# Shifted-window attention block on one core: three placements changed inside the eight-round loop

## Chip, cores and metric

One Trainium2 chip, one core. The metric is the device time of one execution in microseconds (us); lower is better.

## What is computed

The reference is a Swin block on x of 32 x 56 x 56 x 64 floats: LayerNorm, roll by (-3, -3), windows of 7 x 7, eight-headed attention with a position bias and the shift mask, projection, roll back, residual; then LayerNorm, fc1 to 256, GELU, fc2, residual.

```python
y = roll(_ln(x, norm1_w, norm1_b), (-3, -3))           # windows of 49 tokens, 64 channels
q, k, v = split(win @ qkv_w.T)                         # 8 heads of 8
attn = softmax(q @ k.T * scale + bias + mask)
x = shortcut + roll_back(attn @ v @ proj_w.T + proj_b)
z = gelu(_ln(x, norm2_w, norm2_b) @ fc1_w.T + fc1_b) @ fc2_w.T + fc2_b
return x + z
```

## The kernel before, in words

The work is cut into 128 units (NSB). A unit is 16 windows: two rows of eight, the two rows lying in partitions 0 to 48 and 64 to 112. Every engine runs a `body(i, m)` over i with an inner loop of eight rounds, `k` = 0 to 7. A round is one pair of windows per partition half. The order inside a round is written out by hand, and every engine keeps its own order strictly; semaphores tie the engines together. The rest of the block (norms, projections, the MLP) is spread over the eight rounds, each piece for another unit: in pass i the scores are those of unit i; `a` = i+1 has its q, k and v made, `f` = i+2 has its normalised rows turned, `n` = i+3 has its first norm begun; `c` = i-1 has its attention output finished and projected, `d` = i-2 has its second norm, `e` = i-3 its MLP, `g` = i-4 its result.

TensorE (PE), in each round: `scores` (L722, with mask matmuls L726 in some rounds) into the one bank S; `scores_T` (L738) into ST; the extra piece of the round; `shift` (L744), which adds the negated row maxima to ST; `times_v` (L758); in round 4 then `fc2` (L851). The extra pieces: round 0 `project_qk` (L784), round 1 `project_v` (L798), round 2 `fc1_low` and round 3 `fc1_high` (both L829), round 4 `turn_y` (L766, "M<-weights,y"), round 5 `turn_o` (L766, "M<-weights,on"), round 6 `project_out` (L814); at the top of the next round 0 `turn_z` (L766) and `turn_back` (L859). I write S(k) for the first score matmul of round k, and sh(k), V(k) for `shift` and `times_v` of round k.

VectorE (DVE), in each round: `neg_max` (L582), the negated maxima nm of S. PE may write S(k+1) only after nm(k). Extra pieces: round 0 `ln2_sum`, `normalise` of heads (L588, L592), `evac_zT`, then nm, `result` (L634), `ln2_center` (L612); round 1 `low_parts` (L573) and `ln2_var` (L617, L621); round 2 `ln1_sum` (L546); round 3 `ln1_center` (L553); round 4 `normalise` of the second half ahead of nm, then `evac_yT`; round 5 `ln1_var` (L558, L562); round 6 `add_attention` (L600).

GpSimd (POOL), in each round: `shift_rows` (L326), which spreads nm into nmd; sh(k+2) waits for it. Extra: round 0 `keep_residual` (L346) ahead of it, round 1 `ln1_rows` (L339), round 4 `ln2_rstd` and `ln2_rows` (L353, L359), round 7 `ln1_rstd` (L333).

ScalarE (ACT), in each round: `exp` (L426). Extra: round 0 `high_parts` (L407) and `square2`, round 1 `place_v` (L417), round 2 both halves of GELU (L445, with a table load on each side), round 3 `square1`, round 4 `evac_oT`, round 5 `evac_m`.

SyncE issues the DMAs: x in, results out, and per unit sixteen copies of hl into the per-head tiles qp and kp (L274), which the next scores read.

Of the kernel before, what the change touches and what calls it, by code (L numbers as in the profile page):

```python
# [43 lines left out]
def swin_block(nc, x, c_vec, c_weights, c_projb, c_keys, c_diag, c_shift, out):  # L44
    NSB = x.shape[0]
    ctx = ExitStack()
    with ctx:
# [6 lines left out]
        def sem(name):  # L54
            return ctx.enter_context(nc.semaphore(name))
# [127 lines left out]
        s_g = sem("s_g")  # L183
# [12 lines left out]
        def on_chip(u):  # L196
            return not isinstance(u, int) or 0 <= u < NSB

        def later(u, k=1):
            return not isinstance(u, int) or u >= k  # L200
# [11 lines left out]
        def at_unit(i, k, back):  # L212
            return i + (k - back) // U, (k - back) % U
# [271 lines left out]
        def _(dve):  # L485
# [41 lines left out]
            def gather_heads():  # L527
                dve.wait_ge(c_tb, 1)
                then(V.tensor_copy(first[:], S[0:W0 + HEADS, 0:N]))
                for src, lo, hi in ((S[0:W0 + HEADS, N:10 * N], 0, 9), (ST[0:W0 + HEADS, 0, 0:10 * N], 9, 19),  # L530
                                    (ST[0:W0 + HEADS, 1, 0:5 * N], 19, 24)):
                    part = V.tensor_tensor(heads[:, lo:hi, :], src.rearrange("h (k q) -> h k q", q=N),
                                           first[:].unsqueeze(1).broadcast_to([W0 + HEADS, hi - lo, N]), ALU.subtract)
                    part.then_inc(c_heads, 1)

            def place_bias(n, b):
                dve.wait_ge(c_rows_in, 32)
                then(V.tensor_copy(bias_hi[:], bias_t[:]))
                V.scalar_tensor_tensor(bias_rows[:], bias_hi[:], lopart[0:BIAS], bias_t[:], ALU.mult, ALU.add).then_inc(c_bias, 1)
                dve.wait_ge(c_bias, 1)  # L540
                V.tensor_copy(qp[n][b][0:BIAS].rearrange("p h (w q) -> p h w q", q=N),
                              bias_rows[:].unsqueeze(2).broadcast_to([BIAS, HEADS, 8, N])).then_inc(c_q[n][b], 1)

            def ln1_sum(u, r):
                dve.wait_ge(s_x[r % RING], loaded(u, r))
                V.tensor_reduce(sum1[:], xin[r % RING][:], AX_X, ALU.add).then_inc(s_sum1, 1)  # L546
# [24 lines left out]
            def low_parts(u):  # L571
                dve.wait_ge(s_hi, u + 1)
                V.tensor_tensor(hl[:, 1].rearrange("m b a t -> m a b t"),  # L573
                                M[:, 0:2, 0:HT].rearrange("m a (b t) -> m a b t", b=2),
                                hl[:, 0].rearrange("m b a t -> m a b t"), ALU.subtract).then_inc(s_lo, 1)
# [9 lines left out]
            def normalise(u, b):  # L585
                dve.wait_ge(s_pv, U * u + 4 * b + 4)
                o = O[0:R, 0:PAIRS * 4 * VC].rearrange("r (a f) -> r a f", f=VC)
                V.reciprocal(rec[:], o[:, :, 2 * D:VC]).then_inc(s_rec, 1)  # L588
                dve.wait_ge(s_rec, 2 * u + b + 1)
                if b == 0 and later(u):  # L590
                    dve.wait_ge(s_oTp, u)
                V.tensor_tensor(on[:, PAIRS * b:PAIRS * b + PAIRS, :].rearrange("r p (h e d) -> r (p h) e d", e=2, d=D),  # L592
                                o[:, :, 0:2 * D].rearrange("r a (e d) -> r a e d", d=D),
                                rec[:].unsqueeze(3).broadcast_to([R, 4 * PAIRS, 2, D]), ALU.mult).then_inc(s_on, 1)
# [8 lines left out]
            def ln2_sum(u, r):  # L603
                dve.wait_ge(s_att, u + 1)
                V.tensor_reduce(sum2[:], xres[r % RING][:], AX_X, ALU.add).then_inc(s_sum2, 1)
# [9 lines left out]
            def ln2_var(u):  # L615
                dve.wait_ge(s_sq2, u + 1)
                V.tensor_reduce(ss2[:], sq2[:], AX_X, ALU.add).then_inc(s_ss2, 1)  # L617
                dve.wait_ge(s_ss2, u + 1)
                if later(u):
                    dve.wait_ge(s_rs2, u)  # L620
                V.tensor_scalar(veps2[:], ss2[:], 1.0 / C, EPS, ALU.mult, ALU.add).then_inc(s_ve2, 1)  # L621
# [15 lines left out]
            def body(i, m):  # L637
                a, f, n, c, d, e, g = i + 1, i + 2, i + 3, i - 1, i - 2, i - 3, i - 4
                if isinstance(i, int) and i == -2:
                    gather_heads()  # L640
                if isinstance(i, int) and i == 0:
                    place_bias(0, 0)
                for k in range(U):
                    if k == 0:
                        if on_chip(d):
                            ln2_sum(d, m + 2)
                        if on_chip(c):
                            normalise(c, 0)
                        if on_chip(e):
                            evac_zT(e)  # L650
                    if k == 4 and on_chip(c):
                        normalise(c, 1)
                    if on_chip(i):
                        neg_max(i, k)
                    if k == 0:
                        if on_chip(g):
                            result(g, m)
                        if on_chip(d):
                            ln2_center(d, m + 2)
                    if k == 1:  # L660
                        if on_chip(a):
                            low_parts(a)
                        if on_chip(d):
                            ln2_var(d)
                    if k == 2 and on_chip(n):
                        ln1_sum(n, m + 3)
                    if k == 3 and on_chip(n):
                        ln1_center(n, m + 3)
                    if k == 4 and on_chip(f):
                        evac_yT(f)  # L670
                    if k == 5 and on_chip(n):
                        ln1_var(n)
                    if k == 6 and on_chip(c):
                        add_attention(c, m + 3)
# [4 lines left out]
        def _(pe):  # L679
# [121 lines left out]

            def turn_o(u, e, a):
                pe.wait_ge(s_on, 2 * u + 2)
                if not on_chip(e):
                    pe.wait_ge(s_vx, 2 * a + 2)
                turn_tokens(3, on, s_oTp)

# [55 lines left out]
            def body(i, m):  # L863
                a, f, c, d, e, g = i + 1, i + 2, i - 1, i - 2, i - 3, i - 4
                if i == -2:
                    pe.wait_ge(c_weights_in, 16)
                    pe.wait_ge(c_scaled, 1)
                if i == 0:
                    pe.wait_ge(c_const_in, 48)
                for k in range(U):  # L870
                    u2, j2 = at_unit(i, k, 2)
                    r2 = m if k >= 2 else m + 3
                    u4, j4 = at_unit(i, k, 4)
                    r4 = m if k >= 4 else m + 3
                    if k == 0 and on_chip(e):
                        turn_z(e, g, i)
                    if k == 0 and on_chip(g):
                        turn_back(g)
                    if i == -2 and k in (0, 5) or i == 0 and k in (2, 3, 5, 6, 7):
                        keep_running(1)  # L880
                    if i == -1 and k == 5:
                        keep_running(5)
                    if on_chip(i):
                        scores(i, m, k)
                    if k == 1 and on_chip(a):
                        room_for_v(a, e, g)
                    if on_chip(u2):
                        scores_T(u2, r2, j2)
                    if k == 0 and on_chip(a):
                        project_qk(a, d)  # L890
                    if k == 1 and on_chip(a):
                        project_v(a)
                    if k == 2 and on_chip(e):
                        fc1_low(e, a, d)
                    if k == 3 and on_chip(e):
                        fc1_high(e, a, g)
                    if k == 4 and on_chip(f):
                        turn_y(f, e)
                    if k == 5 and on_chip(c):
                        turn_o(c, e, a)  # L900
                    if k == 6 and on_chip(c):
                        project_out(c, f)
                    if on_chip(u2):
                        shift(u2, r2, j2)
                    if on_chip(u4):
                        times_v(u4, r4, j4)
                    if k == 4 and on_chip(e):
                        fc2(e)
# [92 lines left out]
```

## Time and profile before

| what | value |
|---|---|
| median of 3 runs | 2191.48 us (2190.91 to 2192.81) |
| the profiled execution | 2191.34 us, its span 2189.5 us |
| PE matmul busy | 2140.3 us (98%) |
| DVE busy | 1780.1 us (81%) |
| POOL busy | 1772.9 us (81%) |
| ACT busy | 1545.3 us (71%) |
| DMA engines | 28% by the one large queue |
| mean granted TensorE clock | 0.993 of 2.4 GHz |

The trace is read as follows. A row of the timeline is a start, a duration, the engine, the line and the tiles, with a count where neighbours of one kind are merged. A matmul's recorded duration contains the time in which it drains beside its follower, so lengths of pieces on PE are taken from start to start. A row may also contain time in which the instruction had begun but was held. Three engines are over 80% busy, so a wait moved on one of them soon meets a wait of another.

### The profile page before, as it was taken

To read this page: it belongs to the slowest core of one execution; us is meant where nothing else is said; L and a number is where in the kernel's file an instruction comes from. 1 tells how busy PE (TensorE), PEld (TensorE's weight loads), DVE (VectorE), ACT (ScalarE), POOL (GpSimd) and SP (SyncE) were. 2 spreads that over 40 slices of the span, in tenths; PEclk is the share of its full clock that TensorE was granted. 3 is DMA by queue.
4 is the path that set the end of the run, shared out by engine and by line. 5 is a ranking of instruction groups with operands and counts; after the bars stand their busy time and mean duration, and the time that the engine had idled before them with its cause. 6 is when DMAs were issued, how large, how long until landed. Compare 5 with 4: busy or idle time off the path is not lost.

```text
span 2189.5 us, 148006 instructions
## 1 busy us (share of the span) xinstructions
PE 2140.3 (98%) x62790; PEld 1667.7 (76%) x62790; DVE 1780.1 (81%) x3231; ACT 1545.3 (71%) x2435; POOL 1772.9 (81%) x1687
## 2 busy tenths in 40 slices
PE   6999999999999999999999999999999999999997
PEld 3777777777777777777777777777777777777775
DVE  5788888888888888888888888888888888888874
ACT  4577777677677777767777776776777777777774
POOL 5788888888888888888888888888888888888874
PEclk8999999999999999999999999999999999999999
DMA  4232233222323332232323223233223333322321
GB/s 111 65 78 78 75 75 76 77 77 76 79 74 76 76 76 77 75 79 76 77 76 76 77 75 77 78 75 79 75 77 77 76 77 76 77 76 76 77 70 32
DMA packets 178587, 165.86 MB, mean 76 GB/s; under 512 B 21144, under 2 KB 152458, under 8 KB 178074
## 3 DMA queue, kind: packets, MB, share of 16 engines
q1 hardware_dynamic: 178074, 157.60, 28.0%
q8 instruction: 495, 8.11, 1.6%
q14 instruction: 18, 0.15, 0.0%
HBM read 28.99 MB, written 25.77 MB: 25 GB/s over the span
## 4 chain that ended last, share of the span: by engine, by line
PE 88%; DVE 4%; issue 3%; ACT 2%; SPq 2%; DMA 1%; DVEq 0%; POOL 0%; ACTq 0%; POOLq 0%
PE O L758 14%; PE S L722 11%; PE ST L744 10%; PE M L766 9%; PE ST L738 9%; PE M L829 9%; PE M L851 8%; PE M L814 5%; PE M L798 5%; PE M L784 4%; PE M L859 2%; PE S L726 2%; SPq L274 1%; DVE nm L582 1%; ACT gl L445 1%
## 5 line engine op out<-in xcount | busy, mean ns | idle before, releaser
L326 POOL TENSOR_TENSOR nmd<-diag,nm 121x392 f16<-121x392 f16 x1024 | 900.3, 892 | 288.1 <-DVE nm L582 234.1
L582 DVE TENSOR_REDUCE nm<-S 121x8 f16<-121x392 f32 x1024 | 574.3, 561 | 225.7 <-PE S L722 138.3
L426 ACT ACTIVATE pT<-ST 113x392 f32<-113x392 f32 x1024 | 506.9, 496 | 229.7 <-PE ST L744 224.9
L758 PEld LDWEIGHTS O<-vx,pT 113*49 113x49 f32 x16384 | 548.6, 126 | 45.1 <-issue 6.1
L758 PE MATMUL O<-vx,pT 113*49 113x18 f32 x16384 | 522.2, 196 | 3.8 <-issue 1.9
L722 PE MATMUL S<-kp,qp 128*49 128x49 f16 x16384 | 390.7, 186 | 11.0 <-DVE nm L582 7.9
L738 PE MATMUL ST<-qp,kp 128*49 128x49 f16 x16384 | 387.0, 185 | 2.4 <-issue 2.3
L722 PEld LDWEIGHTS S<-kp,qp 128*49 128x49 f16 x16384 | 313.0, 103 | 93.1 <-issue 55.5
L744 PE MATMUL ST<-nmd,shiftw 121*49 121x392 f16 x2048 | 354.4, 342 | 0.2 <-POOL nmd L326 0.2
L738 PEld LDWEIGHTS ST<-qp,kp 128*49 128x49 f16 x16384 | 324.8, 103 | 10.2 <-issue 2.3
L407 ACT ACTIVATE hl<-M 128x784 f16<-128x784 f32 x128 | 105.5, 824 | 309.1 <-PE M L784 229.3
L744 PEld LDWEIGHTS ST<-nmd,shiftw 121*49 121x49 f16 x2048 | 108.7, 102 | 246.8 <-issue 122.5
L346 POOL TENSOR_TENSOR xres<-xin,projb 113x512 f32<-113x512 f32 x128 | 205.2, 1603 | 78.6 <-DVE res L634 78.5
L829 PE MATMUL M<-zT,weights 64*128 64x392 f32 x1024 | 237.9, 540 | 2.0 <-DVE zT L627 1.5
L445 ACT ACTIVATE gl<-M,vec 128x784 f32<-128x784 f32 x256 | 220.0, 911 | 4.0 <-PE M L829 2.5
L353 POOL TENSOR_TENSOR rstd<-veps,mhalf 113x8 f32<-113x8 f32 x128 | 210.8, 1647 | 13.9 <-DVE veps L621 13.9
L333 POOL TENSOR_TENSOR rstd<-veps,mhalf 113x8 f32<-113x8 f32 x128 | 209.7, 1638 | 10.5 <-DVE veps L562 10.5
L851 PE MATMUL M<-gl,weights 128*64 128x392 f32 x1024 | 195.1, 503 | 4.9 <-ACT gl L445 4.9
L417 ACT ACTIVATE vx<-M 49x512 f32<-49x512 f32 x256 | 154.8, 605 | 17.1 <-PE M L798 4.6
L426 ACT ACT_TABLE_LOAD x126 | 161.7, 1283 | 2.2
L445 ACT ACT_TABLE_LOAD x126 | 161.7, 1283 | 2.2
L600 DVE TENSOR_TENSOR xres<-M,xres 113x512 f32<-113x512 f32 x128 | 88.6, 692 | 72.7 <-PE M L814 72.7
(90 smaller groups left out, 3369.2 us busy)
## 6 DMA issues: line engine op xcount, KB each, us to landing
qp<-hl SPq DMA_DIRECT2D x1024, 49.0 KB
kp<-hl SPq DMA_DIRECT2D x1024, 49.0 KB
xin<-in_x SPq DMA_DIRECT2D x256, 98.0 KB
out<-res SPq DMA_DIRECT2D x256, 98.0 KB
kp<-in_c_keys SPq DMA_DIRECT2D x4, 588.0 KB, 7.2
weights<-in_c_weights SPq DMA_DIRECT2D x1, 448.0 KB, 4.4
bias_t<-spread SPq DMA_DIRECT2D x2, 73.5 KB, 2.2
shiftw<-in_c_shift SPq DMA_DIRECT2D x1, 139.0 KB
```

Source lines behind the costliest of these rows:

```text
L326: nc.gpsimd.tensor_tensor(nmd[j % LAG][:], diag[:], nm[j % LAG][:].unsqueeze(2).broadcast_to([RM, 2 * 4, N]), ALU.mult).then_inc(s_nmd, 1)
L333: nc.gpsimd.tensor_tensor(rstd1[:], veps1[:], mhalf[:], ALU.pow).then_inc(s_rs1, 1)
L353: nc.gpsimd.tensor_tensor(rstd2[:], veps2[:], mhalf[:], ALU.pow).then_inc(s_rs2, 1)
L426: nc.scalar.activation(pT[j % LAG][:].rearrange("k w h q -> k (w h q)"), ST[0:R, j % 2, 0:HK], ACT.Exp).then_inc(s_e, 1)
L445: nc.scalar.activation(gl[:, c], M[:, 2 * c:2 * c + 2, 0:HT], ACT.Gelu, bias=b1[:, c:c + 1]).then_inc(s_g, 1)
L582: V.tensor_reduce(nm[j % LAG][:], S[0:RM, 0:HK].rearrange("q (h n) -> q h n", n=N), AX_X, ALU.max, negate=True).then_inc(s_nm, 1)
L722: mm = MM(S[W0 * e:W0 * e + N, N * (4 * w + hp):N * (4 * w + hp + 1)], q[:, 2 * hp + e, t], key[:, 2 * hp + e, t], start=(w == 0 and hp == ...
L738: MM(ST[W0 * e:W0 * e + N, j % 2, N * (4 * w + hp):N * (4 * w + hp + 1)], key[:, 2 * hp + e, t], q[:, 2 * hp + e, t], start=(w == 0 and hp ...
L744: mm = MM(ST[W0 * e:W0 * e + N, j % 2, 0:HK], shiftw[:, variant(r, j), e, :], nmd[j % LAG][:].rearrange("r h n -> r (h n)"), start=False, ...
L758: mm = MM(O[W0 * w:W0 * w + N, (4 * p + hp) * VC:(4 * p + hp + 1) * VC], pT[j % LAG][:, w, hp, :], vx[r % RING][:, window + 2 * w, hp, :], ...
L829: mm = MM(M[:, 2 * c + h, 0:HT], w1[rows, 128 * c:128 * c + 128], zT[rows, :], start=True, stop=True)
L851: mm = MM(M[C * h:C * h + C, 2, 0:HT], w2[:, c, :], gl[:, c, h, :], start=(c == 0), stop=(c == 1), tile_position=(0, C * h), skip_group_ch ...
```

## The change

On PE both halves of fc1 stand in round 3 (the first stood in round 2), and `turn_o` stands right behind `turn_y` in round 4 (it stood in round 5). `turn_o` now waits for both halves of the GELU of unit e, since bank 3 of M is read by the second. On DVE `ln2_var` stands behind nm(2) (it stood behind `low_parts`, ahead of nm(2)), and `ln1_sum` moves from behind nm(2) to behind nm(3), directly ahead of `ln1_center`. No instruction is added or removed.

```diff
@@ DVE body
-                    if k == 1:
-                        if on_chip(a):
-                            low_parts(a)
-                        if on_chip(d):
-                            ln2_var(d)
-                    if k == 2 and on_chip(n):
+                    if k == 1 and on_chip(a):
+                        low_parts(a)
+                    if k == 2 and on_chip(d):
+                        ln2_var(d)
+                    if k == 3 and on_chip(n):
                         ln1_sum(n, m + 3)
-                    if k == 3 and on_chip(n):
                         ln1_center(n, m + 3)
@@ turn_o
                 pe.wait_ge(s_on, 2 * u + 2)
-                if not on_chip(e):
+                if on_chip(e):
+                    pe.wait_ge(s_g, 2 * e + 2)
+                else:
                     pe.wait_ge(s_vx, 2 * a + 2)
@@ PE body
-                    if k == 2 and on_chip(e):
+                    if k == 3 and on_chip(e):
                         fc1_low(e, a, d)
-                    if k == 3 and on_chip(e):
                         fc1_high(e, a, g)
                     if k == 4 and on_chip(f):
                         turn_y(f, e)
-                    if k == 5 and on_chip(c):
+                    if k == 4 and on_chip(c):
                         turn_o(c, e, a)
```

## Rows read from the trace of the kernel before

**Rows 1.** The page's chain that ended last: shares of the span by engine.
```profile
PE 88%; DVE 4%; issue 3%; ACT 2%; SPq 2%; DMA 1%; DVEq 0%; POOL 0%; ACTq 0%; POOLq 0%
```

**Rows 2.** Timeline, PE, one unit: start us, us, engine, line, tiles, count.
```profile
1114.32 0.38 PE L722 MATMUL S<-kp,qp 128*49 128x49 f16 x16
...
1120.19 0.37 PE L722 MATMUL S<-kp,qp 128*49 128x49 f16 x16
...
1122.26 0.40 PE L722 MATMUL S<-kp,qp 128*49 128x49 f16 x16
...
1122.88 0.93 PE L829 MATMUL M<-zT,weights 64*128 64x392 f32 x4
1123.74 0.35 PE L744 MATMUL ST<-nmd,shiftw 121*49 121x392 f16 x2
...
1124.27 0.37 PE L722 MATMUL S<-kp,qp 128*49 128x49 f16 x16
...
1124.90 0.58 PE L766 MATMUL M<-weights,y 113*128 113x113 f32 x4
...
1127.29 0.37 PE L722 MATMUL S<-kp,qp 128*49 128x49 f16 x16
...
1127.81 0.61 PE L766 MATMUL M<-weights,on 113*128 113x113 f32 x4
...
1128.88 0.37 PE L722 MATMUL S<-kp,qp 128*49 128x49 f16 x16
...
1129.30 1.06 PE L814 MATMUL M<-weights,oT 128*49 128x128 f32 x16
...
1130.71 0.38 PE L722 MATMUL S<-kp,qp 128*49 128x49 f16 x16
```

**Rows 3.** Source view of L784, once a unit: median durations, first and last start.
```profile
L784 PE MATMUL M<-yT,weights x512: 489/541/594, 21.1 to 2128.0; 64*128 64x392 f32 x171
```

**Rows 4.** Timeline, DVE, the same unit as Rows 2.
```profile
1120.95 0.78 DVE L621 TENSOR_SCALAR veps<-ss 113x8 f32<-113x8 f32 x1
1121.65 0.55 DVE L582 TENSOR_REDUCE nm<-S 121x8 f16<-121x392 f32 x1
...
1123.27 0.79 DVE L553 SCALAR_TENSOR_TENSOR y<-sum,xin 113x512 f32<-113x512 f32 x1
1124.48 0.36 DVE L588 RECIPROCAL rec<-O 113x32 f32<-113x32 f32 x1 [0.42 <-PE O L758]
1124.87 0.42 DVE L592 TENSOR_TENSOR on<-O,rec 113x256 f32<-113x256 f32 x1
...
1127.70 0.57 DVE L582 TENSOR_REDUCE nm<-S 121x8 f16<-121x392 f32 x1 [1.34 <-PE S L722]
...
1128.90 0.55 DVE L562 TENSOR_SCALAR veps<-ss 113x8 f32<-113x8 f32 x1
```

**Rows 5.** Timeline, ACT, the same unit.
```profile
1121.14 0.50 ACT L426 ACTIVATE pT<-ST 113x392 f32<-113x392 f32 x1
1122.03 0.50 ACT L426 ACTIVATE pT<-ST 113x392 f32<-113x392 f32 x1 [0.39 <-PE ST L744]
...
1123.84 1.72 ACT L445 ACTIVATE gl<-M,vec 128x784 f32<-128x784 f32 x2
```

**Rows 6.** Timeline, PE, near the end, where both fc1 halves follow each other.
```profile
2180.06 1.59 PE L829 MATMUL M<-zT,weights 64*128 64x392 f32 x8 [0.34 <-DVE zT L627]
```

**Rows 7.** Timeline, POOL, the same unit as Rows 2.
```profile
1120.06 1.64 POOL L326 TENSOR_TENSOR nmd<-diag,nm 121x392 f16<-121x392 f16 x2
1121.66 1.05 POOL L339 TENSOR_TENSOR y<-y,rstd 113x512 f32<-113x512 f32 x1
1122.66 2.09 POOL L326 TENSOR_TENSOR nmd<-diag,nm 121x392 f16<-121x392 f16 x2
1125.85 0.84 POOL L326 TENSOR_TENSOR nmd<-diag,nm 121x392 f16<-121x392 f16 x1 [1.10 <-DVE nm L582]
...
1129.38 1.64 POOL L326 TENSOR_TENSOR nmd<-diag,nm 121x392 f16<-121x392 f16 x2
```

## The prediction

> **What bounds the kernel now.** First the chain that ended last: PE holds 88% of it, DVE 4% [rows 1]. So the period of a unit is PE's order of work plus the few waits that PE meets. The last row of that chain says nothing of where these are; the timeline of one unit does. I take a plain unit from S(7) to the next S(7), 1114.32 to 1130.71, that is 16.39 us [rows 2]. Over the whole run L784's 512 matmuls come in 128 groups of four, the first group at 21.1, the last at about 2127.6 (its fourth matmul at 2128.0), so a unit takes 2106.5 / 127 = 16.59 us in the mean [rows 3]; the difference is longer units (one in four has more mask matmuls, and some start late because of the qp and kp copies). All times below are in that trace's clock with the leading 11 left off: 20.19 is 1120.19.
>
> Two waits can be read there. S(3) starts at 22.26, and nm(2) ended at 21.65 + 0.55 = 22.20 [rows 2, 4]: PE was waiting for the maximum, with a latency of 0.06. And turn_y starts at 24.90; the two GELU halves run from 23.84 to 25.56, the first being over at about 24.75 [rows 5]: turn_y was waiting for it. Together they are worth some 0.15 and 0.12 us a unit, estimated from what the same pieces take where nothing is waited for. The change aims at both, so I follow each engine through rounds 2 to 7.
>
> **The terms, and what each engine does in the changed order.** Everything ahead of S(2) is untouched, so S(2) stays at 20.19, and so does what DVE and POOL did up to there.
>
> *Round 2 on PE* loses fc1_low. From a score's start to the piece behind scores_T takes 0.42 (28.88 to 29.30), and sh with V takes 0.53 (23.74 to 24.27) [rows 2]. With no wait S(3) would come at 20.19 + 0.42 + 0.53 = 21.14. But sh(2) needs nmd(0), which POOL makes in the pair from 20.06 to 21.70; its first is over at 20.90 [rows 7]. In the kernel before, fc1_low (0.86: 22.88 to 23.74) covered that; now the cover is gone. sh(2) comes at 20.96, S(3) at 21.49. nm(2) allows it: it starts 0.41 after S(2) (27.29 to 27.70), at 20.60, and ends 0.57 later [rows 2, 4]. So S(3) comes 0.77 earlier than before, 0.86 were removed, and a wait of 0.35 for POOL stands in place of the wait for DVE.
>
> *Round 3 on PE* has both halves. The single one takes 0.86 from start to start; recorded, a single one is 0.93 and both together are 1.59, so the second adds 0.66 [rows 2, 6]. That is a gain of 0.20. S(3) to fc1 is 0.62 (22.26 to 22.88), so fc1 runs 22.11 to 23.63, and S(4) comes at 24.16, against 24.27. scores_T in round 3 needs the exponential that ends at 21.64 [rows 5]; it wants to start at about 21.8, so no wait.
>
> *ACT.* The exponential of round 2 can now follow at about 21.70 instead of 22.03. From its start to the end of the second GELU half took 25.56 - 22.03 = 3.53 [rows 5], so that ends at 25.23, table loads included. Both fc1 halves are done in time for theirs. turn_y wants to start at about 24.16 + 0.51 = 24.67, the first half of the GELU is over at 24.42: that wait goes. turn_o is ready behind it at about 25.1, and must wait for the second half until 25.3 at least.
>
> *DVE.* Here I find what ends last. nm(2) starts at 20.60. From nm through the reduce behind it to the small tensor_scalar takes 1.20 (27.70 to 28.90) [rows 4], so ln2_var's L621 starts at 21.80. Look at what L621 does in the kernel before: it starts at 20.95 and takes 0.78 for eight numbers a partition, to 21.73, and POOL's pair ends at 21.70 [rows 4, 7]. It was held by a POOL instruction in progress and ended 0.03 behind it. At 21.80 it meets ln1_rows, 21.66 to 22.71 [rows 7], and ends at 22.74. nm(3) starts 0.08 before that end, as in the rows, at 22.66. Then ln1_sum, then L553 at 22.66 + 1.20 = 23.86. L553 is the second instruction of this kind: before, it started at 23.27 and took 0.79 to 24.06, where POOL's nmd(2) ended at 23.50, so 0.56 later; and the pair of nmd took 2.09 in place of 1.64, because the second one was held by L553 in its turn [rows 4, 7]. So far L553 came right behind nm(3), before nmd(3) could start. With ln1_sum between them it comes when nmd(3) is running, 23.46 to 24.30, and it ends at 24.30 + 0.56 = 24.86. L588 can start 0.08 earlier, at 24.78. From PE alone it could have started 0.21 behind S(4), at 24.37 (24.48 against 24.27). From L588's start to L592's end is 0.81, so `on` is whole at 25.59, and turn_o starts at 25.65, 0.55 later than PE is ready for it.
>
> The Trainium skill, page "SBUF — State Buffer", section "SBUF: two separate sides", says that a VectorE instruction with two SBUF inputs or in a two-port mode and a GpSimd instruction lock the shared ports against each other for a whole instruction. By that rule both holdings above come out as I have them, and without it L621 and L553 would be short and turn_o would start at 25.3, which is the first rival; the trace agrees with it in the 0.78, the 0.79 and the 2.09.
>
> *Rounds 4 to 7.* From turn_y to S(5) took 2.39 (turn, sh, V and fc2); from turn_o it is as much: S(5) comes at 28.05, against 27.29. Before, turn_o waited for `on` in round 5 and met no wait at all; V(4), which needs `on` too, stood behind turn_y. Now a late `on` is paid in full. Round 5 is empty, only 0.42 + 0.53 = 0.95 long, and S(6) must wait for nm(5): 0.41 + 0.57 + 0.06 = 1.04, so 29.09. Before, S(5) to S(6) was 1.59. S(7) follows 1.83 later (28.88 to 30.71), at 30.92. Against 30.71 the unit is 0.21 us longer.
>
> **What is uncertain in it.** L562 of ln1_var starts 1.61 behind S(5), at 29.66. POOL's nmd(4) starts 0.98 after L592 does (24.87 to 25.85) and nmd(5) 3.53 after nmd(4) (to 29.38) [rows 4, 7]; in the changed order at 26.15 and 29.68. Before, L562 came 0.48 ahead of nmd(5); now it is a dead heat. If L562 comes second, it is held to 30.52 + 0.03, nm(6) starts at 30.47, and S(7) at 31.10 instead of 30.92: 0.18 more. In the one unit of four with more mask matmuls this is hidden, and there the loss is smaller too, as the added matmuls of round 4 fall into the wait for `on`: I take 0.13 (between 0.04 and 0.21). The opposite side: units that start late because of the copies of hl get 0.2 us more slack, and I give back up to 5 us for them, 0 to 8 being the bounds (128 times the 0.06 by which the mean unit exceeds the usual ones). The fill and the drain, some 60 us, have the same pieces; I put them at 0, within 2 us either way.
>
> **Sum.** 96 units x 0.21 + 32 x 0.13 = 24 us. Half of the dead heat: 96 x 0.18 / 2 = 9 us, with 0 and 17 as its ends. Less 5 us. On the profiled execution's 2191.3 us (its span plus 1.8; it lies 0.1 under the median) that gives 2219 us.
>
> **Rivals.** *One: DVE isn't held.* If L621 slips in ahead of ln1_rows (it misses by 0.14 us), nm(3) starts when S(3) allows, about 22.0, L553 at about 23.2 meets nmd(2) as before, and `on` is no later than PE. Then turn_o starts at 25.3 with the GELU, S(5) at 27.70, S(7) at 30.57: 0.14 shorter, in the units with more masks some 0.2. That is 20 us less, 2171 us. For it: a margin of only 0.14 us. Against: L621 was held in the rows when it came less than 0.1 behind a POOL instruction's start. If moreover sh(2) did not wait for nmd(0), 0.3 us more would go, to some 2135 us; the rows of POOL speak against it.
>
> *Two: half held.* L553 or `on` is late by only half of what I have, since one of the steps is off by 0.1 to 0.2 us. Then gain and loss cancel, and the time is 2187 to 2205.
>
> *Three: the dead heat is lost in every unit, and the delay goes on round the ring* (nm(6) late, add_attention late). Then 17 us instead of 9 and no slack given back: 2233, at most 2240.
>
> That the change does not do what it says I leave out: all four moves are moves of whole pieces in a hand-written order.
>
> **Chances.** The forecast (2205 to 2232) 0.55; rival three 0.13; rival two 0.15, of which 0.10 is within 0.2% of 2191.5; rival one 0.17. A difference of 0.2%, 4.4 us, is about what a measurement of this kernel can tell from none. So faster 0.18, within 0.10, slower 0.72. The range reaches from the no-change case to the lost dead heat, 2188 to 2240, and leaves out mainly rival one.
>
> **What would show it.** In the changed trace: sh(2) released by POOL's nmd; L829 as one group of eight with 1.52 from start to next piece; L621 at about 1.0 us and L553 at about 1.0 instead of 0.78 and 0.79; turn_o released by L592 and not by the GELU, some 0.5 us behind turn_y's end; turn_y without a wait; S(6) 1.04 behind S(5), released by nm(5). The prediction is wrong if L553 takes under 0.8, or if turn_o follows turn_y at once.

## The result and the profile after

| what | before | after |
|---|---|---|
| median | 2191.9 us (4 runs, 2190.91 to 2192.81) | 2224.82 us (4 runs, 2220.19 to 2226.24) |
| the profiled execution | 2191.34 us | 2224.78 us, its span 2223.0 us |
| mean granted TensorE clock | 0.993 | 0.993 |

The changed kernel is slower: the ratio is 1.0143, its 95% interval 1.0128 to 1.0159, and the two medians are 33 us apart. The forecast was 28 us more than the profiled execution of before, 2219 us.

The page of the changed kernel, its chain that ended last (shares of the span by engine), against [rows 1]:

```profile
PE 59%; DVE 17%; POOL 11%; issue 9%; SPq 2%; DVEq 1%; ACT 1%; DMA 1%; POOLq 0%; ACTq 0%
```

PE held 88% of that chain before and holds 59% now. What took over is DVE and POOL. The waits of the changed kernel say where (engine, tile and line, releaser: us in total, times, longest us):

```profile
PE M L764 <- DVE on L592: 31.1, 94, 1.1
...
PE ST L742 <- POOL nmd L326: 22.2, 107, 0.9
```

These are the two waits of the prediction, `turn_o` for `on` and `shift` of round 2 for nmd(0). L720, L742 and L764 of this kernel are L722, L744 and L766 of before; L782 is L784.

The same place on PE's timeline, one plain unit of the changed kernel (columns as in [rows 2]). The unit runs from the S(7) at 1112.42 to the one at 1129.23; the last row is the S(7) of the unit after it:

```profile
1112.42 0.38 PE L720 MATMUL S<-kp,qp 128*49 128x49 f16 x16
...
1118.38 0.37 PE L720 MATMUL S<-kp,qp 128*49 128x49 f16 x16
...
1119.15 0.35 PE L742 MATMUL ST<-nmd,shiftw 121*49 121x392 f16 x2 [0.20 <-POOL nmd L326]
...
1119.69 0.37 PE L720 MATMUL S<-kp,qp 128*49 128x49 f16 x16
...
1120.29 1.59 PE L829 MATMUL M<-zT,weights 64*128 64x392 f32 x8
...
1122.34 0.37 PE L720 MATMUL S<-kp,qp 128*49 128x49 f16 x16
...
1122.85 0.61 PE L764 MATMUL M<-weights,y 113*128 113x113 f32 x4
1123.82 0.60 PE L764 MATMUL M<-weights,on 113*128 113x113 f32 x4 [0.36 <-DVE on L592]
...
1126.24 0.37 PE L720 MATMUL S<-kp,qp 128*49 128x49 f16 x16
...
1127.28 0.39 PE L720 MATMUL S<-kp,qp 128*49 128x49 f16 x16
...
1129.23 0.40 PE L720 MATMUL S<-kp,qp 128*49 128x49 f16 x16
...
1145.98 0.40 PE L720 MATMUL S<-kp,qp 128*49 128x49 f16 x16
```

The unit takes 16.81 us: its first S(7) still belongs to a unit with more mask matmuls. The next one, from 1129.23 to 1145.98, is the plain unit with 16.75 us, and that is also the median of the plain units, against 16.39 before [rows 2]. From S(k) to S(k+1), in the rows above:

| step | before | forecast | after |
|---|---|---|---|
| S(2) to S(3) | 2.07 | 1.30 | 1.31 |
| S(3) to S(4) | 2.01 | 2.67 | 2.65 |
| S(4) to S(5) | 3.02 | 3.89 | 3.90 |
| S(5) to S(6) | 1.59 | 1.04 | 1.04 |
| S(6) to S(7) | 1.83 | 1.83, or 2.01 if the dead heat is lost | 1.95 |

These five steps add 0.33. Of the other three only S(7) to S(0) changed, from 2.09 to 2.11 in the medians of the plain units, and with rounding that makes the 0.36.

DVE in the same unit, against [rows 4]:

```profile
1120.07 0.85 DVE L621 TENSOR_SCALAR veps<-ss 113x8 f32<-113x8 f32 x1
1120.84 0.55 DVE L582 TENSOR_REDUCE nm<-S 121x8 f16<-121x392 f32 x1
1121.31 0.67 DVE L546 TENSOR_REDUCE sum<-xin 113x8 f32<-113x512 f32 x1
1122.02 1.02 DVE L553 SCALAR_TENSOR_TENSOR y<-sum,xin 113x512 f32<-113x512 f32 x1
1122.96 0.34 DVE L588 RECIPROCAL rec<-O 113x32 f32<-113x32 f32 x1
1123.34 0.42 DVE L592 TENSOR_TENSOR on<-O,rec 113x256 f32<-113x256 f32 x1
...
1127.85 0.86 DVE L562 TENSOR_SCALAR veps<-ss 113x8 f32<-113x8 f32 x1
```

POOL in the same unit, against [rows 7]:

```profile
1119.85 1.04 POOL L339 TENSOR_TENSOR y<-y,rstd 113x512 f32<-113x512 f32 x1
1120.86 1.64 POOL L326 TENSOR_TENSOR nmd<-diag,nm 121x392 f16<-121x392 f16 x2
...
1127.84 0.84 POOL L326 TENSOR_TENSOR nmd<-diag,nm 121x392 f16<-121x392 f16 x1
```

Read the DVE rows and the POOL rows side by side. L621 ends at 1120.92 and the `ln1_rows` beside it (L339) at 1120.89. L553 ends at 1123.04, the pair of nmd at 1122.50, so 0.54 earlier. L562 ends at 1128.71, nmd(5) at 1128.68; they start within 0.01 us of each other. The eight-number L621 and L562 thus end 0.03 behind the POOL instruction that they meet, and the 512-column L553 0.54, as [rows 4] and [rows 7] had it (0.03 and 0.56). `on` is whole at 1123.76 and `turn_o` starts at 1123.82.

That this is no matter of one unit is told by the source views (count: shortest/median/longest ns, first and last start):

```profile
L553 DVE SCALAR_TENSOR_TENSOR y<-sum,xin x128: 692/1023/1027, 14.6 to 2134.6; 113x512 f32<-113x512 f32 x128
L621 DVE TENSOR_SCALAR veps<-ss x128: 171/857/946, 73.9 to 2208.9; 113x8 f32<-113x8 f32 x128
L562 DVE TENSOR_SCALAR veps<-ss x128: 170/860/870, 16.7 to 2140.4; 113x8 f32<-113x8 f32 x128
```

ACT in the same unit, against [rows 5]:

```profile
1119.33 0.89 ACT L426 ACTIVATE pT<-ST 113x392 f32<-113x392 f32 x2
...
1121.53 1.72 ACT L445 ACTIVATE gl<-M,vec 128x784 f32<-128x784 f32 x2
```

Both halves of the GELU are over at 1123.25, while `on` is whole only at 1123.76. So the wait for the GELU isn't the one that counts.

### The profile page after: what moved, and what is told of

The parts are those of the page before. It is cut to its first block, busy times and chain, and to the rows that moved or that the text cites. A ratio compares the mean times of both kernels' runs of the same rounds, so it can differ in the third digit from the quotient of the medians.

```text
span 2223.0 us, 148132 instructions
## 1 busy us (share of the span) xinstructions
PE 2124.7 (96%) x62790; PEld 1677.2 (75%) x62790; DVE 1847.9 (83%) x3231; ACT 1534.3 (69%) x2435; POOL 1723.3 (78%) x1687
## 4 chain that ended last, share of the span: by engine, by line
PE 59%; DVE 17%; POOL 11%; issue 9%; SPq 2%; DVEq 1%; ACT 1%; DMA 1%; POOLq 0%; ACTq 0%
PE O L756 9%; PE M L851 8%; PE S L720 7%; PE ST L742 6%; POOL nmd L326 6%; PE M L764 6%; PE ST L736 5%; POOL y L339 5%; PE M L814 4%; DVE nm L582 4%; PE M L796 4%; PE M L782 4%; DVE sum L546 3%; DVE y L553 2%; DVE rec L588 2%
## 5 line engine op out<-in xcount | busy, mean ns | idle before, releaser
L326 POOL TENSOR_TENSOR nmd<-diag,nm 121x392 f16<-121x392 f16 x1024 | 850.8, 841 | 371.5 <-DVE nm L582 371.0
L426 ACT ACTIVATE pT<-ST 113x392 f32<-113x392 f32 x1024 | 493.7, 495 | 305.9 <-PE ST L742 301.4
L720 PE MATMUL S<-kp,qp 128*49 128x49 f16 x16384 | 394.4, 186 | 12.7 <-DVE nm L582 5.5
L720 PEld LDWEIGHTS S<-kp,qp 128*49 128x49 f16 x16384 | 312.5, 103 | 97.1 <-issue 61.9
L742 PE MATMUL ST<-nmd,shiftw 121*49 121x392 f16 x2048 | 351.2, 339 | 22.8 <-POOL nmd L326 22.2
L742 PEld LDWEIGHTS ST<-nmd,shiftw 121*49 121x49 f16 x2048 | 108.6, 102 | 193.2 <-POOL nmd L326 100.3
L829 PE MATMUL M<-zT,weights 64*128 64x392 f32 x1024 | 204.6, 515 | 1.6 <-DVE zT L627 1.5
L359 POOL TENSOR_TENSOR z<-z,rstd 113x512 f32<-113x512 f32 x128 | 133.7, 1044 | 10.0
```

Of the source, the lines that this page charges most:

```text
L326: nc.gpsimd.tensor_tensor(nmd[j % LAG][:], diag[:], nm[j % LAG][:].unsqueeze(2).broadcast_to([RM, 2 * 4, N]), ALU.mult).then_inc(s_nmd, 1)
L426: nc.scalar.activation(pT[j % LAG][:].rearrange("k w h q -> k (w h q)"), ST[0:R, j % 2, 0:HK], ACT.Exp).then_inc(s_e, 1)
L720: mm = MM(S[W0 * e:W0 * e + N, N * (4 * w + hp):N * (4 * w + hp + 1)], q[:, 2 * hp + e, t], key[:, 2 * hp + e, t], start=(w == 0 and hp == ...
L742: mm = MM(ST[W0 * e:W0 * e + N, j % 2, 0:HK], shiftw[:, variant(r, j), e, :], nmd[j % LAG][:].rearrange("r h n -> r (h n)"), start=False, ...
```

## The experiments

Each kernel stood beside the kernel before on the same chip, three rounds. A unit is taken here from S(0) to S(0). Every fourth unit has more mask matmuls, and the median is taken for each of the four places in that pattern; "usual unit" below is the mean of these four medians, "plain unit" the median at a place without the added matmuls, and "mean unit" the mean of units 10 to 117. Before: usual 16.53, mean 16.60. After: usual 16.83, mean 16.87.

### e1_dve_only: the two moves on DVE alone

```diff
@@ before: DVE body only
-                        if on_chip(d):
-                            ln2_var(d)
-                    if k == 2 and on_chip(n):
-                        ln1_sum(n, m + 3)
+                    if k == 2 and on_chip(d):
+                        ln2_var(d)
                     if k == 3 and on_chip(n):
+                        ln1_sum(n, m + 3)
```

> The kernel before with the DVE part of the change alone. My theory: nm(2) comes early, but L621 meets ln1_rows and L553 meets nmd(3), so `on` is late by the same amount as in the changed kernel; turn_o still stands in round 5, so only V(4) waits for `on`, for 0.2 us, and PE has fc1_low in round 2 to cover nmd(0). Unit 16.39 + 0.06, time 2198 us (2190 to 2204); L553 at 1.0 us. Rival, the DVE moves are the whole loss: 2215 to 2225.

Measured: 2202.59 us, ratio 1.0057 (1.0040 to 1.0074). DVE in one unit of e1_dve_only:

```profile
1109.15 1.02 DVE L553 SCALAR_TENSOR_TENSOR y<-sum,xin 113x512 f32<-113x512 f32 x1
...
1110.47 0.42 DVE L592 TENSOR_TENSOR on<-O,rec 113x256 f32<-113x256 f32 x1
```

PE in the same unit:

```profile
1110.21 0.58 PE L764 MATMUL M<-weights,y 113*128 113x113 f32 x4 [0.23 <-ACT gl L445]
1110.72 0.35 PE L742 MATMUL ST<-nmd,shiftw 121*49 121x392 f16 x2
1111.04 0.55 PE L756 MATMUL O<-vx,pT 113*49 113x18 f32 x16
```

The time is at the upper end of what was expected. L553 takes 1.02 without any change on PE: the order on DVE makes it. `on` is whole at 1110.89, and V(4) follows at 1111.04; from `shift` to V(4) it is 0.32 and not the 0.18 or 0.19 of the other rounds. So the late `on` is paid in V(4) here, and only in part, because `turn_y` waits 0.23 for the GELU ahead of it.

### e2_pe_only: the moves on PE alone

```diff
@@ before: PE body only
-                    if k == 2 and on_chip(e):
+                    if k == 3 and on_chip(e):
                         fc1_low(e, a, d)
...
-                    if k == 5 and on_chip(c):
+                    if k == 4 and on_chip(c):
                         turn_o(c, e, a)
```

> The kernel before with the PE part of the change alone. My theory: S(3) still waits for nm(2), now for 1.1 us as fc1_low no longer stands in round 2, and turn_o waits for `on`, which comes from V(3), later than before; L553 is short again (0.8). Unit longer by 0.57 to 0.75 us, time 2264 to 2287 us: worse than the changed kernel, so the DVE moves are what makes the PE moves bearable. Rival, the PE moves cost what the changed kernel costs and the DVE moves nothing: 2220 to 2226.

Measured: 2267.2 us, ratio 1.0344 (1.0327 to 1.0361), inside what was expected. PE in one unit of e2_pe_only:

```profile
1104.64 0.37 PE L722 MATMUL S<-kp,qp 128*49 128x49 f16 x16
...
1105.41 0.35 PE L744 MATMUL ST<-nmd,shiftw 121*49 121x392 f16 x2 [0.19 <-POOL nmd L326]
...
1106.71 0.40 PE L722 MATMUL S<-kp,qp 128*49 128x49 f16 x16 [0.61 <-DVE nm L582]
```

S(2) to S(3) is 2.07, as before the change: nm(2) stands behind the held L621, and all of the 0.86 us taken out of round 2 becomes waiting. The 0.66 added in round 3 are then paid in full, and the unit is 17.12. The DVE moves are what lets the PE moves pay anything back; the two parts don't add (75 and 12 us alone, 33 together).

### e3_sum_ahead: L553 comes ahead of nmd(3)

```diff
@@ after: DVE body
-                    if k == 2 and on_chip(d):
-                        ln2_var(d)
+                    if k == 2:
+                        if on_chip(d):
+                            ln2_var(d)
+                        if on_chip(n):
+                            ln1_sum(n, m + 3)
                     if k == 3 and on_chip(n):
-                        ln1_sum(n, m + 3)
                         ln1_center(n, m + 3)
```

> The changed kernel with ln1_sum moved from behind nm(3) to ahead of it (behind ln2_var), so that L553 starts right behind nm(3), before POOL can start nmd(3). If L553's hold is the main cost: L553 at 0.7 us instead of 1.02, nmd(3) longer in turn, turn_o 0.4 us earlier, time 2174 us (2158 to 2182, the lower end if L562 also comes clear of nmd(5)). Rival, `on` is late for another reason (DVE has simply too much to do in round 3, which is the same amount here): 2215 to 2228.

Measured: 2190.12 us, ratio 1.0004 (0.9992 to 1.0015). DVE in one unit of e3_sum_ahead:

```profile
1100.22 0.85 DVE L621 TENSOR_SCALAR veps<-ss 113x8 f32<-113x8 f32 x1
1100.99 0.67 DVE L546 TENSOR_REDUCE sum<-xin 113x8 f32<-113x512 f32 x1
1101.59 0.55 DVE L582 TENSOR_REDUCE nm<-S 121x8 f16<-121x392 f32 x1
1102.06 0.67 DVE L553 SCALAR_TENSOR_TENSOR y<-sum,xin 113x512 f32<-113x512 f32 x1
```

The source views of L553 and L562 over the whole run of e3_sum_ahead:

```profile
L553 DVE SCALAR_TENSOR_TENSOR y<-sum,xin x128: 672/674/1255, 14.6 to 2098.5; 113x512 f32<-113x512 f32 x128
L562 DVE TENSOR_SCALAR veps<-ss x128: 171/856/864, 16.7 to 2104.3; 113x8 f32<-113x8 f32 x128
```

L553 starts before nmd(3) can, takes 0.67, and `turn_o` follows `turn_y` with no wait. The plain unit is 16.34 instead of 16.75: the 0.41 that the late L553 was worth. Not all of that is the hold. From the end of L621 to the end of L553 it is 0.46 less; 0.35 of it is the length of L553, and 0.11 is that L553 no longer stands directly behind the instruction whose result it reads (0.71 from the start of L546 to the start of L553 in the changed kernel, 0.60 from L546 to nm(3) here). L562 stays at 0.86, so that part has another cause (next run). Without the late `on` the changed order is 0.05 shorter than before in a plain unit, so without the late L553 the change would not be slower. The time is another matter. The usual unit fell by 0.40, to 16.43, but the mean unit only by 0.28, to 16.59; the run was foretold at 2174 and missed by 16 us. Some units are longer than usual, and more so than in either kernel. The runs e5, e6 and e11 ask why.

### e4_turn_o_back: turn_o in round 5 again

```diff
@@ after: turn_o, PE body
-                if on_chip(e):
-                    pe.wait_ge(s_g, 2 * e + 2)
-                else:
+                if not on_chip(e):
...
-                    if k == 4 and on_chip(c):
+                    if k == 5 and on_chip(c):
```

> The changed kernel with turn_o back in round 5 (fc1 together, DVE moves kept). My theory: L553 stays at 1.0 us and `on` as late as it was, but only V(4) waits for it (0.3 us), S(6) no longer waits for nm(5), and L562 comes clear of nmd(5): unit 0.29 shorter than the changed kernel's, time 2188 us (2182 to 2196). Rival, the loss lies in round 2 and 3 (the wait for nmd(0)): then 2215 to 2225.

Measured: 2207.26 us, ratio 1.0073 (1.0056 to 1.0090). DVE in one unit of e4_turn_o_back:

```profile
1128.90 1.02 DVE L553 SCALAR_TENSOR_TENSOR y<-sum,xin 113x512 f32<-113x512 f32 x1
...
1130.23 0.42 DVE L592 TENSOR_TENSOR on<-O,rec 113x256 f32<-113x256 f32 x1
...
1134.14 0.66 DVE L562 TENSOR_SCALAR veps<-ss 113x8 f32<-113x8 f32 x1
```

PE in the same unit (the last row is a merged group that the view cuts off):

```profile
1129.81 0.60 PE L764 MATMUL M<-weights,y 113*128 113x113 f32 x4
1130.35 0.35 PE L742 MATMUL ST<-nmd,shiftw 121*49 121x392 f16 x2
1130.80 0.37 PE L756 MATMUL O<-vx,pT 113*49 113x18 f32 x9
```

Two things follow. L562 is clear of nmd(5) again and the dead heat is gone. And V(4) waits for `on` in place of `turn_o`: `on` is whole at 1130.65, V(4) starts at 1130.80, 0.45 behind its `shift` where 0.18 is usual. The wait is about what was foretold (0.27 us for 0.3), but the unit is not: the plain one is 16.57 where 16.46 was expected, and the time missed the expected 2188 by 19 us. Against the changed kernel S(4) to S(5) falls from 3.90 to 3.28, S(5) to S(6) rises from 1.04 to 1.62, and S(6) to S(7) falls from 1.96 to 1.83 (medians of the plain units); with 0.02 behind that, the unit is 0.18 shorter. By the ratios, half of the 1.43% of the change hangs on `turn_o`'s place.

### e5_sum_ahead_hl2 and e6_before_hl2: do late copies make the longer units?

```diff
@@ e3_sum_ahead, and before
-        hl = sb("hl", [128, 2, 2, 2, T // 2], F16)
+        hl = [sb(f"hl{n}", [128, 2, 2, 2, T // 2], F16) for n in range(2)]
...
-                if later(u):
+                if later(u, 2):
...
-                        act.wait_ge(s_q[(r + 1) % 2][b], 64 * u + 64 - 64 * ((r + 1) % 2))
+                        act.wait_ge(s_q[r % 2][b], 64 * u - 64 * (r % 2))
```

With two tiles hl the copies of one unit may still run while the next hl is written; ACT's waits for them, 29 with 80 us in all in the kernel before and 18 with 52 us in the changed one, are gone.

> The run with ln1_sum ahead of nm(3), now with two hl tiles instead of one, so that high_parts waits for the copies of the unit before last. In that run most units take 16.34 us (16.69 with the added mask matmuls), which makes 16.43 in the mean, but the mean was 16.60. If the rest are units in which L407 waited for the copies of hl (93.7 us of such waits in that run's trace, 32 of them), they go: 2168 us (2162 to 2176). Rival, the late units come from something else on PE or POOL: 2186 to 2194.

> Control: the kernel before with two hl tiles. Its mean unit exceeds its usual ones by 0.06 us; if that is the copies, 8 us go: 2182 us (2179 to 2187). Rival, the copies were hidden: 2188 to 2194.

Measured: e5_sum_ahead_hl2 2185.7 us, ratio 0.9993 (0.9982 to 1.0004); e6_before_hl2 2189.13 us, ratio 1.0003 (0.9993 to 1.0013). Both missed: the waits are gone and the longer units are not. The usual unit of e5 is 16.43 and its mean 16.57; those of e6 are 16.53 and 16.59. The copies' waits aren't the cause.

### e7_sum_o_back and e8_sum_o_back_hl2: both causes undone

e7_sum_o_back is e3_sum_ahead with e4's edit on PE; e8_sum_o_back_hl2 is that with two tiles hl.

> ln1_sum ahead of nm(3) and turn_o back in round 5, one hl tile: what remains of the change is fc1 together and ln2_var behind nm(2). S(6) no longer waits for nm(5), L562 comes clear of nmd(5): the usual unit falls from 16.34 to 16.18 us, but the shorter the unit, the oftener L407 waits for the copies. 2178 us (2165 to 2190). Rival, the ring of the copies is the bound: no change against the run with ln1_sum ahead alone, 2186 to 2194.

> The same with two hl tiles: 2153 us (2145 to 2165) if the usual unit is 16.18 us (16.70 with the added mask matmuls) and no unit is late. Rival, another limit takes over (the wait of sh(2) for nmd(0) grows): 2165 to 2180.

Measured: e7_sum_o_back 2181.86 us, ratio 0.9965 (0.9949 to 0.9982); e8_sum_o_back_hl2 2179.42 us, ratio 0.9961 (0.9947 to 0.9974). What is left of the change in e7 is the fc1 pair, `ln2_var` behind nm(2), and `ln1_sum` behind it; it beats both kernels by a little. Source views of e7_sum_o_back:

```profile
L553 DVE SCALAR_TENSOR_TENSOR y<-sum,xin x128: 672/675/1254, 14.6 to 2094.3; 113x512 f32<-113x512 f32 x128
L562 DVE TENSOR_SCALAR veps<-ss x128: 170/622/652, 16.7 to 2099.3; 113x8 f32<-113x8 f32 x128
```

The time of e7 is inside what was expected. The usual unit is 16.38, 0.15 under before; but the mean unit is 16.54, only 0.06 under it. e8 was foretold at 2153 on the theory of the copies and missed by 26 us.

With e7 there are four orders that differ in two things only. Their plain units (medians):

| plain unit, us | L553 late | L553 in time |
|---|---|---|
| `turn_o` in round 4 | 16.75 (changed kernel) | 16.34 (e3) |
| `turn_o` in round 5 | 16.57 (e4) | 16.19 (e7; 16.32 at one of the three plain places) |

So the late L553 costs 0.41 with `turn_o` in round 4 and still 0.38 with `turn_o` in round 5, where V(4) waits for the same `on`. The place of `turn_o` costs 0.15 to 0.18, by the late L562 and the empty round 5. The rest of the change gains 0.20 (16.19 against 16.39). Together that is the 0.36 by which the plain unit grew.

Where the longer units are long can be seen on PE. In one unit of e8_sum_o_back_hl2:

```profile
645.89 0.41 PE L758 MATMUL O<-vx,pT 113*49 113x18 f32 x11
647.26 0.28 PE L758 MATMUL O<-vx,pT 113*49 113x18 f32 x5 [0.95 <-issue]
```

The sixteen matmuls of one V stand in a row in PE's program, with no wait among them, and between the eleventh and the twelfth PE stands still for 0.95 us. I counted such pauses: neighbouring matmuls of one run of scores, scores_T, outputs or projections that start over 0.15 us apart with no wait between, from 200 to 2100 us.

| kernel | pauses | us in all, start to start | (mean less usual unit) x 108 |
|---|---|---|---|
| before | 18 | 7.0 | 8 |
| e6_before_hl2 | 16 | 5.7 | 7 |
| e1_dve_only | 15 | 4.8 | 4 |
| e2_pe_only | 14 | 4.6 | 1 |
| e3_sum_ahead | 36 | 13.0 | 17 |
| e5_sum_ahead_hl2 | 35 | 15.4 | 15 |
| e7_sum_o_back | 29 | 13.1 | 17 |
| e8_sum_o_back_hl2 | 33 | 14.6 | 16 |
| after | 35 | 15.3 | 4 |
| e4_turn_o_back | 36 | 12.9 | 6 |
| e9_after_resid | 39 | 17.3 | 17 |
| e10_resid_sum_o | 32 | 15.2 | 17 |
| e11_half_copies | 19 | 8.8 | 11 |

Where `on` holds PE up (after, e4), the mean unit shows little of the pauses; where hardly anything holds it up (e3, e5, e7, e8, e9), they come out nearly whole. That fits a pause being hidden by the wait behind it: the loss by the late `on` and the loss by pauses overlap, and taking away the first gave only two thirds of its price.

The packed traces say what the pauses wait for. They hold the times of the single packets of the DMA queue named "instruction": some 495 of 16 KB in each kernel, one for about 127 matmuls. Of the 357 pauses in the table 345 end 1.2 to 1.7 us after such a packet has landed, 35 of 35 in the changed kernel and 18 of 18 before; packets come some 4.3 us apart, so for pauses at random moments it would be about one in nine. And all of those 345 packets are late for PE: drawn against the number of matmuls started, each landed behind the mean line (half of them by 25 matmuls or more), while only about half of all packets do.

### e9_after_resid and e10_resid_sum_o: nmd(0) ahead of keep_residual

```diff
@@ after, and e7_sum_o_back: POOL body
-                    if k == 0 and on_chip(i):
-                        keep_residual(i, m)
                     shift_rows(i, k)
+                    if k == 0 and on_chip(i):
+                        keep_residual(i, m)
```

This takes away the other wait of the prediction, that of `shift` in round 2 for nmd(0).

> The changed kernel with keep_residual behind POOL's shift_rows of round 0 instead of ahead of it, so that nmd(0) is ready 2.1 us earlier and sh(2) need not wait for it. If a POOL instruction in progress holds a DVE instruction that reads two tiles, the gain is taken back in part: nmd(0) now runs when L612 starts, so L612 goes from 0.68 to about 0.97 us, square2, place_v and the exponential of round 1 come 0.25 later and scores_T of round 3 waits for it; L621 and L553 end 0.2 earlier, since POOL is ahead. Time 2204 us (2196 to 2214). Rival, no hold: L612 stays at 0.68, and the whole wait of 0.35 us in round 2 goes, but `on` stays late as DVE has the same work: 2220 to 2226.

> keep_residual behind nmd(0), ln1_sum ahead of nm(3), turn_o back in round 5. Compared with the run without the move of keep_residual (2182 us), S(3) comes 0.26 earlier and scores_T of round 3 waits 0.2 for the exponential, whose chain L612's hold makes late: 2176 us (2165 to 2184). Without the hold on L612 both would be gone: 2150 to 2160.

Measured: e9_after_resid 2192.01 us, ratio 1.0011 (0.9998 to 1.0024); e10_resid_sum_o 2187.92 us, ratio 0.9997 (0.9984 to 1.0010). DVE in one unit of e9_after_resid:

```profile
1115.60 1.03 DVE L612 SCALAR_TENSOR_TENSOR z<-sum,xres 113x512 f32<-113x512 f32 x1
...
1119.20 0.40 DVE L621 TENSOR_SCALAR veps<-ss 113x8 f32<-113x8 f32 x1
```

POOL in the same unit, nmd(0):

```profile
1115.25 0.84 POOL L326 TENSOR_TENSOR nmd<-diag,nm 121x392 f16<-121x392 f16 x1
```

The source view of L612 in e9_after_resid:

```profile
L612 DVE SCALAR_TENSOR_TENSOR z<-sum,xres x128: 682/1032/1042, 67.0 to 2176.3; 113x512 f32<-113x512 f32 x128
```

nmd(0) now runs where L612 was alone, and L612 goes from 0.68 in both kernels to 1.03, ending 0.54 behind it. That was foretold (0.97), worked out from L553 alone: the order on POOL makes and moves the hold as well as the order on DVE. What was not foretold is L621: it comes when POOL's `ln1_rows` is nearly over, ends at 1119.60 where that ends at 1119.57, and takes 0.40 for 0.86. So DVE is earlier in rounds 2 to 4 and `on` hardly late, although L553 is still held; the usual unit is 16.50, 0.33 under the changed kernel, and the time 12 us better than expected, 4 us below the range. On top of e7 the same edit is a loss: e10 was foretold at 2176 and took 2187.92, and its ratio of 0.9997 lies above that of e7 with the intervals apart (usual unit 16.41 for 16.38, mean 16.57 for 16.54). S(2) to S(3) falls from 1.31 to 1.12, and S(3) to S(4) rises from 2.65 to between 2.76 and 2.94, as PE now waits there for the exponential (13.8 us in 30 waits over the run, `scores_T` for `exp`).

### e11_half_copies: half the copies left out

```diff
@@ e8_sum_o_back_hl2: spread_parts
+                        if n >= 2 and later(u, 2):
+                            continue
```

From the third unit on half of the copies of hl into qp and kp are left out (and their waits count accordingly), so what is computed is no longer the block; everything else is issued as in e8.

> The run with turn_o back, ln1_sum ahead and two hl tiles (2179 us), with half of the copies of hl left out from the third unit on, so the output is not the block's. Most units of that run take 16.18 us, but the mean is 0.16 us above the usual ones, and its trace shows PE standing still in the middle of runs of matmuls that wait for nothing. If the stream of instructions is starved by the traffic of the copies, these pauses shrink: 2160 us (2153 to 2170). Rival, they have nothing to do with the copies: 2175 to 2184.

Measured: 2172.87 us, ratio 0.9925 (0.9908 to 0.9941); that is between the forecast (at most 2170) and the rival (at least 2175). The page's line of the large queue (packets, MB, share of 16 engines) in the changed kernel; packets and MB are the same in e8 (share 30.0%):

```profile
q1 hardware_dynamic: 178074, 157.60, 28.0%
```

The same line in e11_half_copies:

```profile
q1 hardware_dynamic: 105498, 106.99, 17.6%
```

There are 19 pauses of 8.8 us in all, against 33 and 14.6 in e8: with a third of the traffic gone, four tenths of the pauses go. The usual unit is the same, 16.35, and the time is less by 0.36% of the kernel before, 8 us. So the pauses hang on DMA traffic in part, though not on the waits for the copies. PE's program is written out without loops, and its instructions come by DMA too. The packets above show that a pause ends with such an arrival; that the packets are late because the other queues are busy fits this run, but is argued from it alone. Why the pauses grow when both parts of the change are there (35, against 14 and 15 with one part) stays open.

## Why the prediction was right

**The way and the size.** 2219 us were forecast, 2224.8 measured; the rivals that had it faster or level are out, since L553 took 1.02 and `turn_o` waited 0.36 for `on`.

**Round 2.** Right. `shift` waited for POOL's nmd(0), and S(3) came 1.31 behind S(2) where 1.30 was foretold. e2_pe_only shows what this step rests on: without `ln2_var`'s move S(3) stays at 2.07. e9_after_resid takes the wait away, and the step is 1.12 there and not the 0.95 of a round without any wait: nm(2) ends last then.

**Round 3.** Right: the pair is one group of 1.59, and 2.65 stand for the 2.67 worked out from [rows 6].

**The GELU.** Right: 0.23 of waiting in e1_dve_only, none in the changed kernel.

**DVE held by POOL.** Right, and it is the step that carries the result. L621 and L553 were foretold at about 1.0 each. L553 is 1.02. L621 is 0.85, having started 0.08 later than I had it, and its end is the one foretold to 0.01: what counts is when POOL's instruction ends. The Trainium skill, page "SBUF — State Buffer", section "SBUF: two separate sides", has VectorE and GpSimd share one port pair under an exclusive lock held for whole instructions; these rows agree, with 0.03 and 0.54 us from POOL's end to DVE's. Both are what the instruction takes when it meets nothing (0.17 and 0.67 us) less 0.13 or 0.14, so that POOL's end and that length give the end of the held one. e3_sum_ahead is the test: with L553 ahead of nmd(3) it is 0.67, and the plain unit is 0.41 shorter.

**Rounds 4 to 6.** Right: 3.90 for 3.89, and 1.04 for 1.04, S(6) directly behind nm(5). One side figure was off: `turn_o` was to be 0.55 later than PE was ready for it, and it is 0.40: in e3, where it has nothing to wait for, it starts 0.57 behind `turn_y` (from 1122.85 that is 1123.42, against the 1123.82 measured). The sum did not use it, since the start came from `on`. And the prediction had the late `on` as paid because `turn_o` stands in round 4; the table of e7 shows that V(4) would have paid 0.38 of it with `turn_o` in round 5.

**The dead heat.** This is the term that was mis-sized. I took half of it, 9 us, for a tie that nothing decided. L562 has a median of 860 ns: in the plain units nmd(5) came first throughout. S(6) to S(7) is 1.95, between 1.83 and 2.01: nm(6) starts 1.35 behind S(6), takes 0.55 and S(7) follows 0.05 behind it, where the prediction had 1.38, 0.57 and 0.06. With it the plain unit is 0.36 longer, not 0.21 or 0.30. It hangs on `turn_o` in round 4, which leaves round 5 empty, and not on the late `on`: e3 keeps it, e4 and e7 lose it.

**One unit in four.** It is 17.08 us against 16.93, so 0.15 where 0.13 was taken.

**The slack.** The size was right by luck, since the mechanism was not the one I named. 96 x 0.36 + 32 x 0.15 = 39 us; the mean unit exceeds the usual one by 0.04 instead of 0.075, which gives 4.5 us back, and 39 less 4.5 is 35, against 33.4 between the two profiled executions; the rest is within the 2 us left for fill and drain. I put those 5 us down to copies of hl. e5, e6 and e8 take the copies' waits away and the longer units stay. What the wait for `on` covers is, by the table of pauses, mostly the pauses of PE's own stream; that is argued from the table and not tested by itself.

**Shown and open.** Shown is that the late `on` costs 0.41 us a plain unit (e3), that `turn_o`'s place costs up to 0.18 (e4), and that PE's moves lose on their own and get back through DVE's (e1, e2). PE's pauses end with late packets of instructions; open is why one order of the same instructions has twice as many of them as another.

## What to carry to other kernels

Before moving a small VectorE instruction, look up which GpSimd instruction is running at its new place: an eight-column operation can cost 0.85 us there, and a 512-column one ends half a microsecond behind it. Put such an instruction directly behind the VectorE result that releases GpSimd, so that it starts first. And ask for every consumer moved forward whether its producer had slack: `on` was whole 2.5 us ahead of `turn_o` in round 5 [rows 2, 4] and has no time to spare in round 4. Look at all consumers, though, and not only at the one that was moved: V(4) waits for `on` as well and stood only 0.30 us behind it. With the fc1 pair moved, 0.38 us of the delay came into the period of the loop even with `turn_o` left in round 5 (e4 against e7).

## What the hardware showed that I had not expected

- Which of the two goes first can't be told from the recorded starts alone. In the changed kernel L562 starts 0.03 us before `ln2_rows` ends, nmd(5) follows on POOL without a gap, and L562 ends 0.03 behind nmd(5). In e4 and e7 it starts some 0.6 before that end, and gets in between the two (0.66 and 0.62 us long in the plain units, ending 0.02 or 0.03 behind `ln2_rows`), with nmd(5) no longer than usual.
- The hold counts in the duration. None of these holds appears as idle time in a row; an eight-column instruction of 0.85 us is the only trace of it. Medians against the shortest of the same shape (170 and 857 ns) find it.
- PE can stand still for a microsecond inside a run of matmuls without any wait (0.95 us of idle time in e8), 14 to 39 times a run. The number falls with DMA traffic (33 to 19 when the large queue carries 107.0 MB instead of 157.6), and 345 of 357 such pauses end 1.2 to 1.7 us after a late 16 KB packet of instructions has landed.
